# Moving one PSUM bank from the score ring to the ring of max products: 3 + 3 becomes 2 + 4

## What is computed

```python
attn = jnp.einsum('bhqd,bhkd->bhqk', q, k) / math.sqrt(HEAD_DIM)
attn = attn + alibi_bias(seq_len, N_HEADS)[None] + causal_mask(seq_len)[None, None]
attn = jax.nn.softmax(attn, axis=-1)
y = jnp.einsum('bhqk,bhkd->bhqd', attn, v)
...
x = x + _L0_attn_ref(xn, W_qkv, W_o) + _L0_ffn_ref(xn, wg, W, b)
```

## Time and profile before

| what | value |
| --- | --- |
| three runs | 1753.88, 1758.34, 1759.58 us |
| median | 1758.34 us |
| profiled execution | 1754.4 us, its span 1752.7 us |
| TensorE matmul busy | 1626.1 us, 93% of the span |
| VectorE busy | 1044.3 us, 60% |
| ScalarE busy | 750.1 us, 43% |
| GpSimd busy | 876.1 us, 50% |
| mean granted TensorE clock | 0.962 |

### The profile page before, as it was taken

How to read it: one execution, slowest core, us unless ns; L and a number is a source line. 1 busy time by engine, 2 the same in 40 slices (tenths; PEclk the granted TensorE clock), 3 DMA queues, 4 the chain that set the end, 5 groups by cost and what they waited for, 6 DMA issues and landing times. The chain is left out here.

```text
span 1752.7 us, 26965 instructions
## 1 busy us (share of the span) xinstructions
PE 1626.1 (93%) x9266; PEld 988.5 (56%) x9267; DVE 1044.3 (60%) x2452; ACT 750.1 (43%) x1575; POOL 876.1 (50%) x869
## 2 busy tenths in 40 slices
PE   5999999689599999999999999999999997799898
PEld 4777777544254554554554554554554433588686
DVE  6434332487576776776776776776776700544366
ACT  2222222114354555565555555555555564411110
POOL 4500000006776676676676676676676676223360
PEclk8999999859899999999999999999999998899899
DMA  6655554592901901901901901901900400455595
GB/s 225 222 175 187 179 190 170 151 163 51 163 11 31 172 8 27 176 8 30 173 9 27 176 8 27 177 8 26 177 9 28 184 7 24 164 154 163 197 396 222
DMA packets 98236, 205.68 MB, mean 117 GB/s; under 512 B 11180, under 2 KB 28620, under 8 KB 92476
## 3 DMA queue, kind: packets, MB, share of 16 engines
q1 hardware_dynamic: 84200, 172.26, 38.6%
q0 software_dynamic: 9248, 23.53, 4.3%
q10 hardware_dynamic: 4672, 8.41, 1.7%
HBM read 124.55 MB, written 79.07 MB: 116 GB/s over the span
## 5 line engine op out<-in xcount | busy, mean ns | idle before, releaser
L1115 ACT ACTIVATE probs_sb<-score_ps 128x512 f32<-128x512 f32 (+3 forms) x1280 | 585.0, 552 | 475.8 <-PE score_ps L1187 451.1
L1017 DVE TENSOR_REDUCE part_max<-max_ps 128x1 f32<-128x512 f32 x768 | 473.4, 679 | 211.9 <-PE max_ps L1155 209.9
L1155 PE MATMUL max_ps<-k_aug,q_aug 104*128 104x512 f32 (+3 forms) x1280 | 508.9, 410 | 54.6 <-DMA k_aug<-steps_d 37.4
L1187 PE MATMUL score_ps<-q_aug,k_aug 106*128 106x512 f32 (+4 forms) x1280 | 478.8, 396 | 8.7 <-ACT probs_sb L1115 7.3
L964 POOL TENSOR_TENSOR quad_sum<-probs_sb 128x512 f32<-128x512 f32 x288 | 360.0, 1285 | 164.3 <-ACT probs_sb L1115 141.0
L1155 PEld LDWEIGHTS max_ps<-k_aug,q_aug 104*128 104x128 f32 x1280 | 247.0, 194 | 241.6 <-DVE part_max L1017 86.7
L1187 PEld LDWEIGHTS score_ps<-q_aug,k_aug 106*128 106x128 f32 (+1 forms) x1280 | 241.0, 189 | 145.6 <-ACT probs_sb L1115 122.8
L1231 PE MATMUL acc_ps<-probs_sb,v_sb 128*32 128x512 f32 (+3 forms) x2560 | 291.2, 541 | 0.0
L1013 DVE CUSTOM_DVE_ANT_0 max_ps<-max_ps,mask_row 128x384 f32<-128x384 f32 (+3 forms) x512 | 239.2, 515 | 69.1 <-PE max_ps L1155 68.1
L971 POOL TENSOR_TENSOR quad_sum<-quad_sum,probs_sb 128x512 f32<-128x512 f32 x192 | 239.2, 1283 | 0.0
L980 POOL TENSOR_SCALAR_AFFINE_SELECT probs_sb<-probs_sb 128x512 f32<-128x512 f32 x128 | 80.3, 636 | 207.9 <-ACT probs_sb L1115 207.4
(11 more groups left out here) (177 smaller groups left out, 1753.6 us busy)
## 6 DMA issues: line engine op xcount, KB each, us to landing
k_aug<-k_hi_d SPq DMA_DIRECT2D x14, 1024.0 KB
q_aug<-q_hi_d SPq DMA_DIRECT2D x14, 1024.0 KB
slot_y_d<-y_rows SPq DMA_DIRECT2D x39, 256.0 KB, 2.0
xn_d<-xn SPq DMA_DIRECT2D x8, 1024.0 KB, 5.3
q_hi_d<-st_hi SPq DMA_DIRECT2D x32, 256.0 KB, 3.5
q_lo_d<-st_lo SPq DMA_DIRECT2D x32, 256.0 KB, 3.6
k_hi_d<-st_hi SPq DMA_DIRECT2D x32, 256.0 KB, 2.5
k_lo_d<-st_lo SPq DMA_DIRECT2D x32, 256.0 KB, 2.9
```

What stands on the lines that cost most here:

```text
L1017: nc.vector.tensor_reduce(part_max[:, hh * QT + i, kc:kc + 1], max_ps[:, bank, 0:w], AX.X, ALU.max).then_inc(max_taken, 1)
L1115: nc.scalar.activation(probs[:, r % P_SLOTS, hh, off:CH], score_ps[:, (r * HG + hh) % S_BANKS, off:CH], ACT.Exp).then_inc(exp_done, 1)
L1155: nc.tensor.matmul(max_ps[:, bank, 0:w], q_aug[0:ROW_MAX, half, hh, i * P:(i + 1) * P], k_aug[0:ROW_MAX, half, hh, kc * CH:kc * CH + w], s ...
L1187: nc.tensor.matmul(score_ps[:, u % S_BANKS, off:CH], k_aug[rows, half, hh, jb * P:(jb + 1) * P], q_aug[rows, half, hh, cc * CH + off:(cc + ...
```

## The change

```diff
-S_BANKS, M_BANKS, P_SLOTS = 3, 3, 4
+S_BANKS, M_BANKS, P_SLOTS = 2, 4, 4
```

## The result

| | before | changed |
| --- | --- | --- |
| median of 4 runs | 1756.14 us | 1849.79 us |
| lowest to highest | 1753.88 to 1759.58 | 1848.93 to 1851.19 |
| ratio, 95% interval | | 1.0525 [1.0507, 1.0543] |
| span of the profiled execution | 1752.7 us | 1849.2 us |

What follows compares the result with a forecast made beforehand. TensorE's in-order queue was taken to bound the attention, with ScalarE saturated within a phase. Middle groups +72, last group +18 and first group -3 gave +87 us on 1754.4, taken as 1842 us, range 1798 to 1882.

Steps and rivals of the forecast that it cites:

- the turn of a score bank: Score ring: one bank's cycle takes 1.24 us, so two banks give one score per 0.62 us, slower than ScalarE's 0.504.
- Off-diagonal phases: Middle groups, M0's load to M7's in twelve visits a group: 4.55 us against 3.69, costing +10.3 us a group.
- Visits with 512 and 384 columns: Three diagonal visits a middle group: phase 4.40 us against 3.74 and a mean of 3.61, costing +2.4 us a group.
- Visits with 256 and 128 columns: Three diagonal visits a middle group, set by VectorE: the fourth max bank gains 0.3 us each, -0.9 a group.
- merged start: Fourth pair of diagonal visits of a group, 16 scores and 16 maxima: 8.1 us against 7.93, +0.2.
- Middle groups: Six groups between first and last: +12.0 us each, +72 us in all, nothing given back by the products.
- First group: VectorE sets its phases; the score chain limits the gain to about 4.9 us a phase: -3 us, bounds -10 and +4.
- Last group: +18 us: +3 from its first visits, +9.5 from thirteen visits of scores alone, +5 from falls of the clock.
- the clock's two terms: Last group: +5 us for three clock falls in thinner score-only visits; -2 for a vanished wait of 1.64 and its fall.
- Rival A: Score ring: two banks suffice with a turn of at most 1.01 us, -35, so 1720 us; chance 0.05.
- Rival B: Whole kernel: the chain costs less and the max ring's gain cancels it, within 5 us of before; chance 0.04.
- Rival C: Middle groups: the clock falls in one visit in five, products take twice as long, +60, about 1905 us; chance 0.08.

Runs made afterwards that it cites:

- experiment 5: The changed kernel (two score, four max banks) with Exp handling only the first 256 columns of a tile (128 where the diagonal leaves fewer): 1762.48 us.
- experiment 10: The kernel before with one score bank, three max banks and two PSUM banks idle: 2862.65 us.
- Experiment 1: The kernel before with two score banks, three max banks and one PSUM bank idle: 1863.15 us, ratio 1.0614.
- experiment 9: The kernel before with an unread matmul added behind most scores of the last group from round 14 on: 1753.41 us against 1753.82, ratio 0.9992.
- experiment 4: The kernel before (three and three banks) with Exp handling only the first 256 columns of a tile (128 where the diagonal leaves fewer): 1735.85 us.
- Experiment 8: The changed kernel with an unread matmul added behind each score of the last group's visits without maxima, from round 16 on: 1838.66 us, ratio 1.0495.
- experiment 7: The kernel before (three and three banks) with all but the last of a visit's row-sum and value pieces moved between its scores: 1783.42 us, ratio 1.0176.

## Why the prediction was right, point by point

- **The cause.** Taking three banks to two makes the turn of a score bank (0.63 + 0.61 = 1.24) the pace of the phase. The turns in the changed trace are 1.19 and 1.25, and experiment 5 shortens the turn and takes most of the loss away; experiment 10 has the same turn with one bank. No row stood behind the 0.11 us from a matmul's end to its Exp: in the visit shown it is 0.65 us from Exp 0 to the load of S2 and 0.54 from there to Exp 2, so the way back was put slightly too short and the way forward slightly too long.
- **Off-diagonal phases.** Forecast 4.55 against 3.69. The 72 of the middle groups have 4.43 to 4.80, 4.56 on their mean, and 4.51 in the visit shown.
- **Visits with 512 and 384 columns.** Forecast 4.40, measured 4.30 to 4.33.
- **Visits with 256 and 128 columns.** Forecast -0.3 each; measured -0.4 each in five of the six middle groups (3.26, 3.21 and 3.46 against 3.67, 3.61 and 3.86); in the first of them the second is 3.49. Experiment 1 shows that the gain belongs to the fourth max bank. The merged start was forecast at 8.1 and is 8.09 in these five, 8.36 in the first.
- **Middle groups.** +72 forecast, +70.5 measured, and nothing given back: from the last load of a phase to the next phase it takes 2.58 us on the mean off the diagonal, where it took 2.53.
- **First group.** -3 forecast, -1.6 measured, but not as one effect. Its visits of 5.2 to 5.5 us fell to 4.85 to 5.15, near the forecast limit of 4.9 by the score chain. One visit went the other way: its first score waited for the rows of maxima, and its phase is 9.98 us instead of 4.74. This wait is not the change's alone: with three and three banks the same phase is 6.06 us in experiment 9 and 7.35 in experiment 4. So the sum came out near the forecast by effects that were not in it.

```profile
402.43 0.28 PEld L1187 LDWEIGHTS score_ps<-q_aug,k_aug 106*128 106x128 f32 x1 [3.39 <-DMA q_aug<-max_lo]
```

- **Last group: the term that was mis-sized.** The thirteen phases of scores alone grew by 12.9 us where the sum had about 11, and the six phases with maxima by 2.7 where it had 3. The products behind them, though, grew by 10.3 us (47.5 against 37.2), where the clock's two terms (+5, and -1.6 out of the -2) gave 3.4. The wait of 1.64 us and the fall behind it did vanish, as forecast. For the others I took three falls of the clock, at 1.6 us each. In the trace eight of the twelve product parts are longer than before, by 0.4 to 2.0, and the clock is between 0.57 and 0.78 in six of the eight windows of 10 us from 1470 to 1550. Experiment 8 shows that it is the clock: with it held up, 10 us come back. A fall was priced right, experiment 9 takes 1.6 us each out of two; their number was a guess, and too low.
- **Rival A** (faster) needed a turn under 1.01 us. Experiment 5 has about 1.0, and there 67 of the 94 us are gone, though the time is still longer and not shorter; the real Exp is too long for it. The rule of the Trainium skill that stood behind this rival (Perfetto Trace Analysis, "Matmuls": rotate through different banks so that one is drained while the next is written) names no number. Two banks rotate as well, and they were not enough here.
- **Rival B** (no difference) is excluded by the same turns.
- **Rival C** (the clock falls in the middle groups) did not happen with two banks: the window from 560 to 1420 us, below, has a granted clock of 1.00. Two short falls lie in it, at 899.9 and 1329.9 us, and the kernel before has two as well, at 572.3 and 835.1. With one bank the clock did fall (experiment 10).

```profile
560.00:1420.00 860.00, 816.91 (x5060) 394.80 (x5056) 592.53 (x1464) 484.45 (x1008) 538.12 (x480) 1.00 0.34 65
```

- **The rule on the most contended engine** (the Trainium skill, Perfetto Trace Analysis, "Identifying the Most-Contended Engine") would have given the bank to VectorE, which is busier. The measurement decides against it here: at 3 + 3 ScalarE, busy 43% of the span, was saturated within the phases, and at 2 + 4 the ring in front of it set them. By experiment 1 the bank taken from ScalarE's ring costs 109 us, and given to VectorE's it brings 15.5 back.

**What stays open.** Why the products between the phases became about 0.1 us a visit longer in experiment 5 than in its control, and what the moved pieces of experiment 7 gained against their 5.5 us a group. No run separates these.

## What to carry to other kernels

Measure the turn of a PSUM bank in the trace: from the start of the instruction that drains it to the load that it releases, and from that load to the next drain. Turn divided by banks must be below the pace that the slower of the two engines sets while the ring is in use: here 1.24 / 3 = 0.41 us was below ScalarE's 0.504, and 1.24 / 2 = 0.62 was not. A share of the span says nothing on it. A bank that keeps a ring under this pace is worth far more (109 us here) than one that shortens the waits of a ring that is already there (15.5), and the loss can be computed before anything is built.

## What the runs showed of the hardware

- The granted clock fell in stretches that have no long wait. In the changed kernel's middle groups, with one max and one score per 0.62 us in the phases, it was 1.00 over 860 us. In its last group, with one score alone per 0.62 us, it fell again and again (0.57 to 0.78), and in experiment 10, with a max and a score per 1.2 us, too (0.68 over 1300 us). The longest wait of a weight load within these phases was 1.06 us in the last group and 1.23 in experiment 10; the first load behind a visit's products waited at most 1.66.
- Added matmuls that nobody reads made the last group of the changed kernel 10 us shorter (experiment 8).
- In the changed kernel a 128x512 Exp and the next matmul into its bank take 0.65 us from the Exp's start to the weight load, and 0.54 us from that load to the next Exp.
- Eight narrow product matmuls take 0.86 us ahead of others of their kind (kernel before), and 1.00 us ahead of a full-size weight load (experiment 7).
